# A gated delta rule inside an eight-stage network: new order of its step, and the two stages around it as pipelines

## The chip, the cores and the metric

One NeuronCore of one Trainium2 chip runs the whole network as one program. The metric is the device time of one execution in microseconds, lower is better. All tensors are float32.

## What is computed

Eight layers follow one another, each as `x = x + layernorm(f(layernorm(x)))`, on `x` of shape (8, 512, 128). The change touches only the fifth, the gated delta rule attention. Cut to what matters:

```python
h = silu(conv(rmsnorm(x)) + conv_b)            # causal depthwise convolution, width 4
q, k, v = h @ q_w, h @ k_w, h @ v_w            # 16 heads of 64; q and k normalised
alpha, beta = sigmoid(h @ alpha_w + alpha_b), sigmoid(h @ beta_w + beta_b)
def step(s, inp):                              # scan over 512 tokens, state 64 x 64 per head
    qt, kt, vt, at, bt = inp
    s = s * at[..., None]
    u = einsum('bhd,bhdv->bhv', kt, s)
    s = s + bt * (kt[..., None] * (vt - u)[..., None, :])
    return s, einsum('bhdv,bhd->bhv', s, qt)
y = rmsnorm_per_head(outs)
gate = sigmoid(silu(x @ u1_w + u1_b) @ u2_w + u2_b)
y = x + y @ out_w * gate
y2 = rmsnorm(y)
y = y + silu(y2 @ ff_w1) * (y2 @ ff_w3) @ ff_w2
```

## The kernel before

The core runs eight stages in turn. Between two stages all engines meet at a barrier, and a stage's weights are loaded at its start (`issue_loads`, L102). The fifth layer is three stages. Within a stage each engine runs its own instruction stream in the order written; the streams meet only through semaphores (`wait_ge`, `sem_clear`, `then_inc`).

**The stage ahead, `stage_delta_in` (L1683).** A loop over 8 batches of 512 tokens. VectorE takes the statistics (L130, L133), GpSimd makes the inverse root (L143, L144), VectorE applies it (L155), and the same again for the inner norm (L153). TensorE turns the result (L1721), ScalarE copies it out (L1748), VectorE convolves it in four instructions (L1777, L1779), ScalarE applies SiLU twice (L1754, L1755), TensorE projects the betas in 32 small matmuls (L1730), VectorE adds the bias (L1785), ScalarE applies the sigmoid (L1758), and only then does VectorE begin the next batch. At the end VectorE clears `xn` (L1794).

**The stage of the delta rule, `stage_delta` (L1798).** A loop over 65 turns; one turn, called a step here, is one pair of heads of one batch (8 batches by 8 pairs, and one turn more to end the pipeline). The two heads of a pair lie in the two halves of the 128 partitions, so nearly all matmuls are 64 rows by 64 columns of the array, one head in the quadrant of rows and columns 0 to 63, the other in the quadrant of 64 to 127. The scan is done in chunks of 64 tokens, whose triangular systems are solved by doubling over five levels: at level `l`, `gram(l)` (L2026) forms products of keys, VectorE masks them into `N` and `AT` (`masked`, L2417, L2418), `z_step(l)` (L2055) multiplies `N` by the inverse `T` so far, ScalarE copies `Z` out (L2323), `t_step(l)` (L2069) multiplies again, ScalarE copies `T` (L2316) and VectorE transposes it (L2425). GpSimd scales the keys for the next Gram: `carry(l)` waits for Gram `l`, then scales `kd` (L1914) and `k` (L1908), and its `lv_ready` lets TensorE begin Gram `l + 1`. VectorE hears of a Gram through GpSimd (`gr_fwd`). Between these lie four links of the chain along the sequence: `solve(t)` (L2103 to L2107), copy of `U` (L2329), `state_and_output(t)` (L2117 to L2124), `state(t)` on VectorE (L2437), `from_state(t+1)` (L2137, L2141), `residual` (L2445). The projections of the next step and the output of the one before are spread between them: `project_qk` (L2151), `square_sums` (L2161), `project_gates` (L2167), `key_norms` (L2175), `project_v` (L2182), `head_sums` (L2193), `output` (L2202), and the cross Gram (L2043). At the end of a step are `keys_by_tokens` (L2212), and at its start `gram(0)`, `cross_z` (L2079), `diagonal` (L2014), `cross_t` (L2090). The order on TensorE is the function `step()`. It is written out 5 times (`UNROLL = 5`) in a loop of 13 turns. The other engines loop over single steps.

**The stage behind, `stage_delta_out` (L2567).** A loop over 8 batches: norm of `x`, two gate matmuls (L2614, L2619) with SiLU and sigmoid between them, the gated sum on VectorE (L2692, L2693), inner norm, turn (L2624), four pairs of up products (L2632, L2633), SiLU (L2672), product (L2704), down product (L2641), sum (L2709), the post norm and the sum into `x` (L293). Only the norm of the next batch's input is brought forward.

Of the kernel before, what the change touches and what calls it, by code (L numbers as in the profile page):

```python
# [16 lines left out]
P = 128  # L17
TB = L // P
# [1664 lines left out]
def stage_delta_in(core):  # L1683

    st = Stage(core, "d")
# [3 lines left out]
    pre = Pre(st, inner="rms", eps=DELTA_EPS)  # L1689
    pad = KCONV - 1  # L1690
    hp = st.sb("hp", [P, pad + L])
    cv = st.sb("cv", [P, 2, L])
    hs = st.sb("hs", [P, L])
    bt = st.sb("bt", [P, NC, NPAIR])
    t_ready, t_free = s("pre_t_ready"), s("pre_t_free")
    hp_ready, cv_ready, hs_ready, hs_free = s("conv_in_ready"), s("conv_ready"), s("hs_ready"), s("hs_free")
    b_ps, b_ready, b_done, bank_free = s("beta_ps"), s("beta_ready"), s("beta_done"), s("beta_bank_free")
    with nc.Block() as block:
# [4 lines left out]
        @block.gpsimd  # L1703
        def _(g):
            ch = Chain(g, core.lasting_sem("pool_chain"))
            with g.Fori(0, B) as b:
                ch.reset()
                pre.pool(g, ch, b)

        @block.tensor  # L1710
        def _(pe):
            st.wait_loads(pe)
            pe.sem_inc(pre.y_free, 1)
            pe.sem_inc(hs_free, 1)
            with pe.Fori(0, B) as b:
                pe.wait_ge(pre.y_ready, 1)
                pe.sem_clear(pre.y_ready)
                pe.wait_ge(t_free, 1)
                pe.sem_clear(t_free)
                for t in range(TB):  # L1720
                    r = pe.transpose(c.ps[7][:, t * P:(t + 1) * P], pre.y2[:, t, :], c.ident[:])  # L1721
                r.then_inc(t_ready, 1)
                pe.drain().then_inc(pre.y_free, 1)
                pe.wait_ge(hs_ready, 1)
                pe.sem_clear(hs_ready)
                pe.wait_ge(bank_free, 1)
                pe.sem_clear(bank_free)
                for u in range(NC):
                    for h in range(2):
                        r = pe.matmul(c.psum[h * DH:(h + 1) * DH, 6, u * NPAIR:(u + 1) * NPAIR], hs[:, u * CH:(u + 1) * CH],  # L1730
                                      bw[:, h * NPAIR:(h + 1) * NPAIR], start=True, stop=True)
                r.then_inc(b_ps, 1)
                pe.drain().then_inc(hs_free, 1)
            pe.wait_ge(t_free, 1)
            pe.sem_clear(t_free)
            pe.wait_ge(bank_free, 1)
            pe.sem_clear(bank_free)

        @block.scalar
        def _(a):  # L1740
            ch = Chain(a, core.lasting_sem("act_chain"))
            st.wait_loads(a)
            a.sem_inc(t_free, 1)
            with a.Fori(0, B) as b:
                ch.reset()
                a.wait_ge(t_ready, 1)
                a.sem_clear(t_ready)
                a.activation(hp[:, pad:], c.ps[7], ACT.Identity, scale=gamma[:]).then_inc(hp_ready, 1)  # L1748
                a.drain().then_inc(t_free, 1)
                a.wait_ge(cv_ready, 1)  # L1750
                a.sem_clear(cv_ready)
                a.wait_ge(hs_free, 1)
                a.sem_clear(hs_free)
                a.activation(c.xT[:, bass.ds(b * L, L)], cv[:, 1, :], ACT.Silu, bias=cb[:])  # L1754
                a.activation(hs[:], cv[:, 1, :], ACT.Silu, bias=cb[:]).then_inc(hs_ready, 1)  # L1755
                a.wait_ge(b_ready, 1)
                a.sem_clear(b_ready)
                ch.link(a.activation(c.beta[:, :, bass.ds(b * TB, TB), :],  # L1758
# [1105 lines left out]
```

## Time and profile before

| | |
|---|---|
| median of 3 runs | 6820.89 us (6817.22 to 6825.5) |
| the profiled execution | 6872.23 us, its span 6870.4 us |
| `stage_delta_in` | 182.6 us |
| `stage_delta` | 2717.8 us |
| `stage_delta_out` | 276.9 us |
| the other seven layers | 3693.1 us |
| granted TensorE clock, whole span | 0.869 of 2.4 GHz |

Times are microseconds unless marked ns. PE is TensorE's matmuls, PEld its weight loads, DVE is VectorE, ACT ScalarE, POOL GpSimd. A float32 matmul of the source is two records of the profile, each with its weight load. "Idle before" a record is the time in which that engine had nothing running, with the engine that ended it. A wait for several semaphores is put down to one of them. Matmul ends are modelled, so durations of a group of matmuls are best read from the start of one group to the start of the next.

### The profile page before, as it was taken

What the parts mean: (1) busy time and instruction counts of PE and PEld (TensorE: products, weight loads), DVE (VectorE), ACT (ScalarE), POOL (GpSimd) and SP (SyncE); (2) the same over time, 40 slices, a digit from 0 to 9 for tenths busy, and PEclk for the clock granted to TensorE, in tenths of its full rate; (3) what the DMA queues carried; (4) which work ended last, traced back from release to release, by engine and by line L of the source; (5) the groups of instructions that cost most, each with busy time, mean ns of one, the idle gap of its engine ahead of it and who ended that gap; (6) DMA issues with size and microseconds to landing.
All of it is one profiled execution on the core that took longest, in us unless ns stands there. A gap on an engine that the chain in (4) does not pass through costs nothing.

```text
span 6870.4 us, 180526 instructions
## 1 busy us (share of the span) xinstructions
PE 5324.7 (78%) x70660; PEld 3956.2 (58%) x70660; DVE 3447.2 (50%) x9349; ACT 2368.9 (34%) x4122; POOL 2561.7 (37%) x2842
## 2 busy tenths in 40 slices
PE   4568758888719999999999999997579996111998
PEld 3434435555417877787777787786246664101676
DVE  4531357777634444444444444444445555676433
ACT  3432236666523333333333333333223332000333
POOL 2210014444315555555555556554100002675000
PEclk8789879999859899999999999998789998555999
DMA  0000000000000000000000000000010000000000
GB/s 17 0 17 0 2 37 1 0 0 0 0 6 12 11 11 11 11 11 11 11 11 12 11 10 11 11 13 11 0 37 0 0 0 3 0 0 25 0 0 12
DMA packets 29512, 57.41 MB, mean 8 GB/s; under 512 B 7312, under 2 KB 14240, under 8 KB 28704
## 3 DMA queue, kind: packets, MB, share of 16 engines
q1 hardware_dynamic: 28960, 48.86, 2.2%
q8 instruction: 492, 8.06, 0.5%
q14 instruction: 60, 0.49, 0.0%
HBM read 46.75 MB, written 2.10 MB: 7 GB/s over the span
## 4 chain that ended last, share of the span: by engine, by line
PE 52%; DVE 9%; POOL 3%; another core or an unknown queue 3%; issue 2%; ACT 1%; DVEq 0%; POOLq 0%; ACTq 0%
PE psum L617 7%; PE psum L607 7%; PE psum L2055 5%; PE psum L2026 5%; PE psum L2069 3%; PE psum L600 3%; PE psum L2167 2%; PE psum L2151 2%; PE psum L2161 2%; DVE e_sq L2470 2%; PE psum L2043 1%; POOL a_pv L1480 1%; PE psum L2202 1%; PE psum L2182 1%
## 5 line engine op out<-in xcount | busy, mean ns | idle before, releaser
L617 PEld LDWEIGHTS psum<-m_wd,m_h 128*128 128x128 f32 x6144 | 812.8, 194 | 485.3 <-issue 484.1
L617 PE MATMUL psum<-m_wd,m_h 128*128 128x128 f32 x6144 | 825.5, 278 | 91.2 <-remote 64.4
L1914 POOL TENSOR_TENSOR e_kd<-e_kd,e_tail 128x512 f32<-128x512 f32 x325 | 369.5, 1137 | 694.1 <-PE psum L2026 680.8
L607 PE MATMUL psum<-xT,m_wa 128*128 (+1 forms) x1032 | 552.7, 618 | 8.5 <-remote 8.5
L607 PE MATMUL psum<-xT,m_wb 128*128 (+1 forms) x1032 | 540.4, 606 | 0.0
L784 DVE SCALAR_TENSOR_TENSOR m_acc<-psum,m_combine,m_acc 128x128 f32<-128x128 f32 x1440 | 403.4, 342 | 223.3 <-PE psum L617 209.5
L544 POOL TENSOR_TENSOR m_h<-m_td,m_tb 128x512 f32<-128x512 f32 x258 | 328.5, 1273 | 487.1 <-DVE m_tb L812 487.1
L2055 PEld LDWEIGHTS psum<-e_T,e_N 64*64 64x64 f32 x10400 | 336.0, 137 | 217.6 <-issue 216.6
L2026 PE MATMUL psum<-e_kd,e_k 64*64 64x64 f32 x10400 | 375.7, 223 | 49.4 <-DVE e_AT L2418 49.3
L2055 PE MATMUL psum<-e_T,e_N 64*64 64x32 f32 x10400 | 371.9, 222 | 43.6 <-remote 43.6
L2026 PEld LDWEIGHTS psum<-e_kd,e_k 64*64 64x64 f32 x10400 | 343.5, 138 | 57.8 <-issue 56.4
L143 POOL TENSOR_SCALAR m_post_rstd<-m_post_mv 128x4 f32<-128x4 f32 x27 | 6.1, 228 | 991.5 <-DVE m_post_mv L133 991.5
L607 PEld LDWEIGHTS psum<-xT,m_wb 128*128 128x128 f32 x1032 | 202.6, 196 | 258.5 <-issue 258.5
L805 DVE SCALAR_TENSOR_TENSOR m_h<-psum,m_bb,m_ta 128x512 f32<-128x512 f32 x258 | 193.2, 749 | 309.4 <-ACT m_ta L705 306.2
L705 ACT ACTIVATE m_ta<-psum,m_ba 128x512 f32<-128x512 f32 x258 | 177.2, 687 | 459.7 <-PE psum L607 459.6
L1908 POOL TENSOR_TENSOR e_k<-e_k,e_tail 128x256 f32<-128x256 f32 x390 | 283.4, 727 | 121.9 <-PE psum L2043 121.9
L2323 ACT ACTIVATE e_Z<-psum 128x256 f32<-128x256 f32 x325 | 124.5, 383 | 574.5 <-PE psum L2055 572.0
L2316 ACT ACTIVATE e_T<-psum 128x256 f32<-128x256 f32 x325 | 126.0, 388 | 556.7 <-PE psum L2069 556.7
L2069 PE MATMUL psum<-e_Z,e_TT 64*64 64x32 f32 x8320 | 283.8, 219 | 0.0
L2069 PEld LDWEIGHTS psum<-e_Z,e_TT 64*64 64x64 f32 x8320 | 276.6, 136 | 4.4
L699 ACT ACTIVATE m_h<-psum,m_ba 128x512 f32<-128x512 f32 x258 | 177.3, 687 | 287.0 <-PE psum L600 287.0
L600 PE MATMUL psum<-m_normed,m_wa 128*128 128x512 f32 x516 | 268.5, 603 | 6.3 <-remote 6.3
(412 smaller groups left out, 11727.5 us busy)
## 6 DMA issues: line engine op xcount, KB each, us to landing
e_w<-in_e_w SPq DMA_DIRECT2D x66, 321.0 KB, 2.8
m_wa<-in_m_wa SPq DMA_DIRECT2D x12, 512.0 KB, 7.2
m_wd<-in_m_wd SPq DMA_DIRECT2D x12, 512.0 KB, 8.7
m_wb<-in_m_wb SPq DMA_DIRECT2D x8, 512.0 KB, 9.0
f_h<-in_f_h SPq DMA_DIRECT2D x2, 1024.0 KB
out<-x SPq DMA_DIRECT2D x1, 2048.0 KB, 8.7
f_w<-in_f_w SPq DMA_DIRECT2D x3, 256.0 KB
g_w<-in_g_w SPq DMA_DIRECT2D x3, 256.0 KB
```

The lines of the kernel that those rows point to most:

```text
L544: g.tensor_tensor(h[:, j, :], td[:, j, :], tb[:, j, :], ALU.mult).then_inc(h_ready[j], 1)
L600: pe.matmul(c.ps[u % 4][:], wa[q][:, j, :], nrm[:, e % 2, :], start=True, stop=True).then_inc(a_ready[u % 4], 1)
L607: pe.matmul(c.ps[i][:], w[q][:, j, :], xb, start=True, stop=True).then_inc(a_ready[i], 1)
L617: r = pe.matmul(c.ps[4 + e % 2][:, t * P:(t + 1) * P], h[:, u % DEPTH, t * P:(t + 1) * P], wd[u // UQ][:, u % UQ, :], start=(m == 0 and t ...
L699: a.activation(h[:, j, :], c.ps[u % 4][:], ACT.Relu, bias=ba[:, u:u + 1]).then_inc(h_ready[j], 1)
L784: r = v.scalar_tensor_tensor(to[:, t, :], c.ps[4 + e % 2][:, t * P:(t + 1) * P], comb[:, t, e:e + 1], acc[:, t, :], ALU.mult, ALU.add)
L805: v.scalar_tensor_tensor(h[:, j, :], c.ps[2 * k + 1][:], bb[:, u:u + 1], ta[:, j, :], ALU.add, ALU.mult).then_inc(h_ready[j], 1)
L1908: return g.tensor_tensor(even(k[:], m), even(src[:], m), gate, ALU.mult)
L1914: return g.tensor_tensor(both_odd(dst[:], m), both_odd(src[:], m), gate.unsqueeze(1).broadcast_to((P, 2, nb, m)), ALU.mult)
L2026: r = pe.matmul(c.psum[half(h), G_, chunk(u)], keys[half(h), chunk(u)], both_odd(gated[half(h), :, chunk(u)], m), start=True, stop=True)
L2055: r = pe.matmul(c.psum[half(h), Z_, u * HC:(u + 1) * HC], N[half(h), l - 1, chunk(u)], even(T[half(h), chunk(u)], 1 << l), start=True, sto ...
L2069: r = pe.matmul(even(c.psum[half(h), T_, chunk(u)], 1 << l), left[half(h), chunk(u)], Z[half(h), u, :], start=False, stop=False, skip_grou ...
```

## The change

**Stage ahead.** The loop over batches is written out as a pipeline. Buffers are doubled (`hp`, `cv`, `y2`, two PSUM banks each for turning and betas). VectorE interleaves the first norm of batch `b + 2`, the second part of batch `b + 1` and the convolution of batch `b`. SiLU is applied once, and the betas are projected from `xT`. One sigmoid over all batches at the end takes the place of eight. `xn` is cleared on GpSimd.

**The step.** `z_step(l)` and `gram(l + 1)` (for `l = 5` the cross Gram) become one function `z_and_gram(l)`, whose matmuls alternate. `Z` of a head is written to the other half of the PSUM partitions, so it uses the quadrants that the Gram leaves free. ScalarE copies one half of `Z` back, VectorE the other. The order of the step on TensorE, ScalarE and VectorE is new, and `UNROLL` is 13.

**Stage behind.** The loop is written out. First all gates of the 8 batches are made, with one sigmoid over all; then the gated sums run on GpSimd, three batches ahead; up products run one batch ahead of down products.

```diff
-    UNROLL = 5
+    UNROLL = 13
...
+            def z_and_gram(l):
+
+                pe.wait_ge(n_ready, 1)
+                pe.sem_clear(n_ready)
+                pe.wait_ge(t_ready, 1)
+                pe.sem_clear(t_ready)
                 pe.wait_ge(lv_ready, 1)
                 pe.sem_clear(lv_ready)
                 pe.wait_ge(gr_free, 1)
                 pe.sem_clear(gr_free)
...
                 for u in range(NC):
                     for h in range(2):
-                        r = pe.matmul(c.psum[half(h), Z_, u * HC:(u + 1) * HC], N[half(h), l - 1, chunk(u)],
+                        r = pe.matmul(c.psum[half(1 - h), Z_, u * HC:(u + 1) * HC], N[half(h), l - 1, chunk(u)],
                                       even(T[half(h), chunk(u)], 1 << l), start=True, stop=True)
-                r.then_inc(z_ps, 1)
+                        if u + 1 == NC:
+                            r.then_inc(z_ps[h], 1)
+                    if l + 1 < LEVELS:
+                        r = gram_chunk(l + 1, k, kd, u)
+                    elif u % 2:
+                        r = cross_block(u // 2)
+                r.then_inc(gr_ps, 1)
...
-                scaled_gram(1)
+                gram(1, k, kd, gr_free, gr_ps)
                 solve(0)
-                z_step(1)
                 state_and_output(0)
-                scaled_gram(2)
                 from_state(1)
+                z_and_gram(1)
+                solve(1)
                 t_step(1)
-                solve(1)
                 pe.wait_ge(out_free, 1)
                 pe.sem_clear(out_free)
                 project_qk()
-                z_step(2)
                 state_and_output(1)
-                scaled_gram(3)
                 from_state(2)
+                z_and_gram(2)
+                square_sums()
                 t_step(2)
                 solve(2)
-                square_sums()
+                z_and_gram(3)
                 project_gates()
...
+            def z_copy():
+
+                v.wait_ge(z_ps[1], 1)
+                v.sem_clear(z_ps[1])
+                v.tensor_copy(flat(Z[half(1)]), c.psum[half(0), Z_, 0:NC * HC]).then_inc(z_ready[1], 1)
```

VectorE's loop in the stage ahead, and TensorE's in the stage behind, after the change:

```python
            for b in range(B):
                if b + 1 < B:
                    third(b + 1)
                if b + 2 < B:
                    first(b + 2)
                conv(b)
                if b + 2 < B:
                    second(b + 2)
                if b >= 1:
                    betas(b - 1)
...
            for b in range(B):
                if b + 1 < B:
                    up(b + 1)
                if b + 2 < B:
                    turn_sums(b + 2)
                down(b)
```

## Rows read from the trace of the kernel before

**Rows 1.** Busy time by stage: start:end, length, busy and count, clock, DMA

```profile
1859.20:2041.80 182.60, 23.94 (x288) 20.06 (x288) 66.25 (x250) 39.21 (x48) 20.22 (x32) 0.50 0.00 0
2041.80:4759.60 2717.80, 2470.59 (x55182) 2136.09 (x55182) 1265.79 (x3082) 921.26 (x2020) 1580.62 (x1909) 0.92 0.04 11
4759.60:5036.50 276.90, 139.82 (x532) 81.55 (x532) 109.64 (x388) 75.65 (x98) 31.60 (x50) 0.71 0.01 3
```

**Rows 2.** Timeline of a batch in the stage ahead: start, length, record, idle before

```profile
1885.50 0.87 DVE L130 BATCH_NORM_STATS2 d_pre_stats<-x 128x6 f32 x4 [2.68 <-remote]
1888.47 1.12 DVE L155 TENSOR_SCALAR d_pre_y<-x,d_pre_mv,d_pre_rstd 128x128 f32 x4 [1.69 <-POOL d_pre_rstd L144]
1896.76 2.33 DVE L1779 SCALAR_TENSOR_TENSOR d_cv<-d_hp,d_cw,d_cv 128x512 f32<-128x512 f32 x3
1902.30 1.89 PE L1730 MATMUL psum<-d_betaw,d_hs 128*64 128x8 f32 x32 [7.01 <-remote]
```

**Rows 3.** VectorE's copy of TX, once a step: all 65, and two neighbours

```profile
L2512 DVE COPY e_TX<-psum x65: 424/443/459, 2082.2 to 4721.4; 128x256 f32<-128x256 f32 x65
...
3278.43 0.45 DVE L2512 COPY e_TX<-psum 128x256 f32<-128x256 f32 x1
...
3326.75 0.42 DVE L2512 COPY e_TX<-psum 128x256 f32<-128x256 f32 x1 [1.30 <-PE psum L2090]
```

**Rows 4.** Chain that ended last, where TensorE's loop turns: start, length, what

```profile
3315.48 4.37 another core or an unknown queue
...
3321.70 1.02 issue
```

**Rows 5.** Timeline of one step: TensorE's waits, and GpSimd's carry

```profile
2161.57 1.15 PE L2026 MATMUL psum<-e_kd,e_k 64*64 64x64 f32 x32 [0.93 <-DVE e_AT L2418]
2162.99 1.29 POOL L1914 TENSOR_TENSOR e_kd<-e_kd,e_tail 128x512 f32<-128x512 f32 x1 [1.15 <-PE psum L2026]
2163.70 1.12 PE L2055 MATMUL psum<-e_T,e_N 64*64 64x32 f32 x32 [0.64 <-remote]
2164.24 0.74 POOL L1908 TENSOR_TENSOR e_k<-e_k,e_tail 128x256 f32<-128x256 f32 x1
2164.65 0.43 PE L2117 MATMUL psum<-e_U,e_ket 64*64 64x64 f32 x8
2170.76 1.02 ACT L2293 ACTIVATE e_sq<-psum 128x1024 f32<-128x1024 f32 x1 [1.83 <-PE psum L2151]
2183.59 0.33 PE L2103 MATMUL psum<-e_bv,e_TTH 64*64 64x64 f32 x4 [0.84 <-DVE e_bv L2445]
```

**Rows 6.** Matmuls of other stages on several tiles; the third row is L1002 alone

```profile
73.63 1.09 PE L1002 MATMUL psum<-a_kz,a_qT 64*32 64x512 f32 x16
74.65 0.74 PE L1022 MATMUL psum<-a_vz,a_probsT 128*32 128x18 f32 x64
73.70:73.80 0.10, 0.10 (x8) 0.10 (x16) 1.00 0.00 0
```

**Rows 7.** Busy time and clock (the third number from the end) of three short stretches

```profile
3319.90:3325.90 6.00, 4.94 (x89) 4.85 (x91) 2.08 (x3) 1.42 (x3) 0.00 (x0) 0.50 0.02 5
3381.60:3385.00 3.40, 3.40 (x5) 1.16 (x5) 0.17 (x1) 0.00 (x0) 2.76 (x1) 0.54 0.00 0
2176.80:2178.70 1.90, 1.90 (x6) 0.70 (x5) 0.17 (x1) 0.00 (x0) 1.22 (x1) 1.00 0.00 0
```

**Rows 8.** Timeline of the stage behind: its start, and one batch

```profile
4766.96 0.87 DVE L130 BATCH_NORM_STATS2 g_pre_stats<-x 128x6 f32<-128x128 f32 x4 [7.80 <-DMA g_gamma<-in_g_gamma]
...
4798.40 1.02 PE L2632 MATMUL psum<-g_y2T,g_w 128*128 128x512 f32 x2
...
4799.26 1.02 PE L2633 MATMUL psum<-g_y2T,g_w 128*128 128x512 f32 x2
...
4801.64 3.83 PE L2641 MATMUL psum<-g_w,g_hid 128*128 128x128 f32 x32 [0.92 <-remote]
```

**Rows 9.** Groups by shape in the stage behind: busy, mean ns, idle before

```profile
L2664 ACT ACT_TABLE_LOAD x8 | 10.3, 1283 | 32.3 <-DVE g_gate L2688 32.3
```

More of the change, by code:

```diff
@@ L1739, in _ @@
+                r.then_inc(b_ps[i], 1)
+            turn(0)
+            for b in range(B):
+                if b + 1 < B:
+                    turn(b + 1)
+                betas(b)
+            for i in range(2):
+                pe.wait_ge(b_read[i], 1)
+                pe.sem_clear(b_read[i])
         @block.scalar
         def _(a):
-            ch = Chain(a, core.lasting_sem("act_chain"))
             st.wait_loads(a)
[L1743 to L1758, printed above, removed]
-                                     bt[:].rearrange("p (t h) a -> p a t h", h=2), ACT.Sigmoid))
-                a.sem_inc(b_done, 1)
@@ new lines, in betas @@
+            def betas(b):
+                i = b % 2
+                v.wait_ge(b_ps[i], 1)
+                v.sem_clear(b_ps[i])
+                r = v.tensor_tensor(bt[:, b * NC:(b + 1) * NC, :], c.ps[6 + i][:, 0:NC * NPAIR].rearrange("p (u a) -> p u a", u=NC),
+                                    bb[:].unsqueeze(1).broadcast_to((P, NC, NPAIR)), ALU.add)
+                r.then_inc(b_read[i], 1)
+                return r
+            first(0)
+            second(0)
+            third(0)
+            first(1)
@@ L1795, in stage_delta_in @@
+            second(1)
+            for b in range(B):
+                if b + 1 < B:
+                    third(b + 1)
[6 more added lines that the diff above has]
+                    betas(b - 1)
+            betas(B - 1)
+            v.drain().then_inc(b_ready, 1)
     st.ctx.close()
@@ L2644, in _ @@
+            up(0)
+            turn_sums(1)
+            for b in range(B):
+                if b + 1 < B:
+                    up(b + 1)
+                if b + 2 < B:
+                    turn_sums(b + 2)
+                down(b)
             for i in range(2):
@@ L2675, in _ @@
+            copy_sums(0)
+            for b in range(B):
+                silus(b)
+                if b + 1 < B:
+                    copy_sums(b + 1)
         @block.vector
@@ new lines, in _ @@
+            gate_sum(B - 2)
+            gate_sum(B - 1)
+            sums_stats(0)
+            sums_norm(0)
+            sums_stats(1)
+            hidden(0)
+            sums_norm(1)
+            sums_stats(2)
+            for b in range(B):
+                if b + 1 < B:
+                    hidden(b + 1)
+                if b + 2 < B:
+                    sums_norm(b + 2)
+                if b:
+                    finish(b - 1)
+                result(b)
+                if b + 3 < B:
+                    sums_stats(b + 3)
```

501 lines of the change are left out of this document (286 added, 215 removed).

## The prediction

> **What bounds the kernel now.** I read the busy times by stage first [rows 1]. Three stages are touched: 182.6, 2717.8 and 276.9 us, 3177.3 of 6870.4. The seven other layers' 3693.1 us stay. The reader is to see two kinds of stage. In the stage ahead and the one behind no engine is busy: 66 of 182.6 us for the busiest in the first, 140 of 276.9 in the last, with the clock at 0.50 and 0.71. They are chains of single instructions, each waiting for the one before. In the delta stage TensorE is busy 2471 of 2718 us, so what shortens it is TensorE work or TensorE's waits.
>
> Next I read the timeline of one batch [rows 2, 8], the times of one recurring instruction [rows 3], and the chain of waits through a step and over the turn of the loop [rows 4]. The copy of TX is seen 65 times from 2082.2 to 4721.4, 41.24 us a step. Of the 64 intervals between neighbours, 52 are inside TensorE's loop body, 37.4 to 42.4 us with mean 39.6. The 12 at the turn of its loop are 45.1 to 50.2, mean 48.2; one is 3278.43 to 3326.75. There the chain shows 4.37 and 1.02 us in which TensorE has nothing to run [rows 4], and the six microseconds after it have a clock of 0.50 [rows 7]. A turn thus costs 48.2 - 39.6 = 8.6 us.
>
> **The stage ahead.** One batch's work on VectorE is, from starts in the timeline: first norm's statistics 1.3 (0.87 and 0.38 with gaps), its application and the second statistics 2.8, second application 1.0, convolution 2.9 (0.48 + 2.33), beta sum 0.3: 8.3 us. What goes is the round trip: TensorE's 7.01 us and its kin, one SiLU [rows 2], and 7 sigmoids with their 1.28 us table loads, as in [rows 9]. GpSimd's root takes 1.69 us from statistics to application. `first` is covered by the convolution, but `third(b+1)` comes right after `second` and `betas`, so 1.69 - 0.33 = 1.3 us of it stays each time. Prologue: 1.3 + 1.7 + 2.8 + 1.7 + 1.0 + 1.3 + 1.7 + 2.8 = 14.3. Six full turns of 9.6 = 57.6. The last two batches 5.5 + 3.2. The end (SiLU, 1.89 of TensorE, bias, table 1.28, a sigmoid of 512 columns 0.7) 5.9. Loads at the start 3.6. Sum 90 against 182.6: **92 us gone**, 80 to 102 by whether the roots are hidden and whether GpSimd's clearing of `xn` (3.5 us on VectorE before) holds up its second root.
>
> **The stage behind.** Loads 7.4 us [rows 8]. Gates of 8 batches: VectorE needs 1.3 + 1.1 + 0.7 and 0.5 of root wait, 3.6 a batch; TensorE's turn and two products 2.8 at the full clock, 5.0 at half. I take 4.3, 34 in all, and 5 of fill. One sigmoid of 4096 columns: 0.42 us for each 512 (the ScalarE record of 1024 columns is 1.02 [rows 5], that of 512 0.60) and a table load 1.28 [rows 9], 4.9. Then gated sum 2.6 on GpSimd (1.27 each), statistics 1.9, root 1.7, application 0.9, turn 1.3, copy 0.9: 9.3. First up products, clock half low, 8.5. From there TensorE sets the pace: 7 up products of 8 x 0.86 (4798.40 to 4799.26) = 48.2, 8 down products of 3.8 = 30.4, turns 3.6. VectorE does `result` and `sums_stats` (3.9 us) behind each down product before it frees the banks that the third pair of up products waits for; four matmuls (3.4) cover part, and 1.5 us a batch stays, 10.5. Tail 6.3. Sum 168: **109 us gone**, 150 to 200 by the clock.
>
> **The step: matmuls beside one another.** Z is 32 records and a Gram 32, and each takes 0.94 to 0.98 us from start to start (2163.70 to 2164.65 in [rows 5]), 29 ns a record, whether 32 or 64 columns stream. So a pair of quadrants is bound by its own loads and streams, not by columns. Is it the quadrants or the issue of instructions? Two rows of the first layer tell: 64 records of 128 x 32 begin and end in 0.74 us, at most 12 ns each; and L1002, on 2 x 4 tiles of 64 x 32, has 8 matmuls and 16 weight loads in the same 0.1 us, and ends 16 records of 512 columns in 1.09 us [rows 6]. Issue allows 12 ns, and tiles in both rows and columns run together. Z then hides beside the Gram: 1.0 us for both instead of 1.9. No row has four tiles of 64 x 64, so the bounds are 0.94 (each quadrant's own time) and 1.9 (no gain). I take 1.0, being nearest to L1002. Five times a step: 4.5 us less TensorE work.
>
> The Trainium skill (TensorEngine Tiling (Array Packing), Gotcha 1: PSUM Pressure) speaks against it: different row tiles cannot access the same PSUM bank at once. Both heads' Z lie in one bank, as both heads' Gram do. By that rule the two heads of the old Gram would take turns; but two records of 512 columns in a row on one tile fit in L1002's 1.09 us, so 64 columns stream in 55 to 68 ns, and 29 ns a record is possible only when the heads run together. With four tiles the rule could still bind, and give the first rival below.
>
> **The step: waits.** TensorE's waits in a plain step of 38.16 us are 1.06 before Gram 1 (it shows as 0.93), 0.79 before Z, 0.84 before solve 3 and some 0.6 in small ones [rows 5], 3.3 in all, so 34.9 of work; less 4.5 is 30.4. Now each link of the sequence loses the work that covered it. I walked the new order, Gram 1 at 0, with the latencies of the rows: 0.44 from TensorE to GpSimd, 0.28 to 0.30 to ScalarE, 0.39 to VectorE's `state`, 0.15 to 0.28 back. Gram 1 ends at 0.98, solve 0 at 1.33; the U copy ends at 1.89, so the state products begin at 2.09 (0.76 idle); S is copied by 2.93, `from_state(1)` runs 3.08 to 3.53 (0.4 idle). GpSimd's two scalings (1.29 + 0.74) end at 3.41, and `z_and_gram(1)` begins at 3.69 (0.16). Its Z copies take until 5.5, solve 1 covers part (0.5). The output sums free the banks at 6.6 (0.2 before `project_qk`). `from_state(2)` waits 0.44 for S; `z_and_gram(3)` comes 0.5 early for T 2, `from_state(3)` 0.44 for S, `z_and_gram(4)` 0.5 for T 3. From there to the end nothing waits. Before Gram 1 the old 0.9 stays, since its chain (ket, k, GpSimd 0.84 + 1.50) is unchanged and the diagonal behind `cross_t` fills the wait. Sum 4.8; two more changes between tile shapes, 0.15 each. Step: 30.4 + 4.8 + 0.3 = 35.4. GpSimd's work a step is near 25 us and VectorE's 22, so neither becomes the bound.
>
> **The clock.** Plain intervals without a slow phase are near 38.1, and the mean is 39.6, so slow phases cost 1.5 us a step: the gate products behind the square sums take 3.4 us at a clock of 0.54 and 1.9 at 1.00 [rows 7]. The square sums and head sums stay, so I keep 1.5, between 0 and 4: denser matmuls and more gaps pull both ways. Step 36.9.
>
> **UNROLL** 13 leaves 5 turns of the loop, 4 jumps back instead of 12: 8 x 8.6 = 69 us. Its cover is none, it stands on TensorE's path. The Trainium skill (Runtime: NRT & Kernel Launch, Instruction fetch mechanics) says that a taken branch outside the buffered pages must fetch first; the trace agrees, with 4.37 us at each turn and none within the 5 steps.
>
> Delta stage: 64 x 36.9 = 2362, 4 x 8.6 = 34, the start and last step 76: 2472, **246 us gone**.
>
> **Sum.** 92 + 109 + 246 = 447. The profiled execution was 6872.2 (1.8 around its span), so 6425; it is 51 us above the median of the runs, so 6374 us in the median. Its own range by the bounds (step 33.9 to 38.9, which is 128 us either way at most, the stages 20 and 30) is 6270 to 6500.
>
> **Rivals.** (1) *Four quadrants do not overlap.* The pair stays at 1.9, some 0.3 of waits are covered by it, step 41.1, stage 64 x 41.1 + 34 + 78 = 2742, 24 more than before. With the two outer stages: 6872 + 24 - 201 - 51 = 6644. For it: no row with this shape, and the page's rule. Against: L1002. (2) *The gaps let the clock fall.* After the idle at the loop's turn everything runs at half clock for 6 us [rows 7]. The new step has gaps of 0.4 to 0.8 in its first 7 us. The step must reach (2718 + 201 - 34 - 78) / 64 = 43.9 us for the whole to be slower: 7.0 more than I say, 14 us more of each step at 1.2 GHz. At 45 us it would be 6890. Against: gaps of 0.6 to 0.9 follow each other already at Gram 1 and Z, and that stretch has a full clock. (3) *Only the outer stages gain less*, because unrolled code and GpSimd's gated sums keep their chains: 60 and 60 instead of 92 and 109 would give 6455; this lies in the range.
>
> **How the numbers follow.** My forecast with its range 0.70 (of which a twentieth below 6290), the first rival or a partial overlap 6500 to 6660 0.24, the second 0.04, anything that ends within noise 0.02. The range takes in the first rival: 6270 to 6660. Faster by over 0.2% (13.6 us, what this measurement can tell) 0.94, within 0.01, slower 0.05; the second rival makes nearly all of the last.
>
> **What would show it.** `z_and_gram` in 1.0 us for 64 records, against 1.9; TX copies 36.9 apart, four of them with about 8.6 more; the stage ahead in 90 and the one behind in 168 us; waits of 0.4 to 0.8 before the state products and `from_state`. The forecast fails if the records beside each other stay at 29 ns, if the clock in the stage falls well under 0.92, or if another engine's wait (VectorE's half of the Z copy stands behind `residual` and, at level 2, behind `rest`) holds up every level.

## The result and the profile after

The changed kernel takes 6558.68 us in the median (6549.27 to 6568.25, 4 runs) against 6823.19 (6817.22 to 6829.8, 4 runs): a ratio of 0.9612, 95% interval 0.9595 to 0.963. That is 264 us faster, where 447 were forecast; it lies inside the stated range (6270 to 6660), 185 us above its point. It lies above 6500, where the forecast's own range ended; the range reached further only to take in the first rival, and that rival did not occur.

The profiled execution has a span of 6566.4 us. By stage (start:end, length, busy time and count of PE, PEld, DVE, ACT, POOL, then clock, DMA share, GB/s), answering to [rows 1]:

```profile
1849.40:1940.00 90.60, 23.95 (x288) 20.07 (x288) 63.02 (x248) 14.96 (x19) 28.02 (x34) 0.50 0.01 1
1940.00:4479.70 2539.70, 2249.34 (x55182) 1823.45 (x55182) 1487.52 (x3407) 912.50 (x2020) 1605.25 (x1909) 0.93 0.04 12
4479.70:4736.10 256.40, 158.27 (x528) 93.69 (x528) 96.40 (x360) 42.20 (x60) 51.17 (x64) 0.71 0.01 4
```

The stage ahead fell from 182.6 to 90.6 us, as forecast (90). The delta stage fell by 178 us, not 246. The stage behind, forecast at 168, is 256.4, only 20.5 less than before, although VectorE, ScalarE and GpSimd together have 27 us less to do in it. The other layers are 3679.7 us, 13 less, with no edit in them. Over the traces of all kernels here they take some 3677 to 3697 us, so these 13 are scatter.

The recurring copy of TX in the changed kernel (min/median/max ns, first and last start), answering to [rows 3]:

```profile
L2564 DVE COPY e_TX<-psum x65: 424/447/471, 1978.8 to 4440.7; 128x256 f32<-128x256 f32 x65
```

Its 64 intervals fall into 60 inside the loop body, 35.96 to 40.62 us with mean 38.04 (before 39.6), and 4 at a turn, mean 44.81, so a turn now costs 6.8 us. The forecast had 36.9 and 8.6.

One pair of Z and Gram on TensorE in the changed kernel (start, length, line, tile), answering to the Gram and Z of [rows 5], which took one after the other what is here in one:

```profile
2747.19 0.25 PE L2097 MATMUL psum<-e_T,e_N 64*64 64x32 f32 x2
2747.20 0.27 PE L2067 MATMUL psum<-e_kd,e_k 64*64 64x64 f32 x2
...
2748.13 0.23 PE L2067 MATMUL psum<-e_kd,e_k 64*64 64x64 f32 x2
2748.18 0.28 PE L2152 MATMUL psum<-e_bv,e_TTH 64*64 64x64 f32 x4
```

From 2747.19 to 2748.18 are 0.99 us for 64 records, 15.5 ns each. Forecast: 1.0. The pairs of the higher levels take 1.09 to 1.10 us at the full clock; a group of another tile shape follows each of them.

Where the stage behind lost its gain is seen in two stretches. First its loop over the gates in the changed kernel, one round:

```profile
4511.13 1.11 PE L2690 MATMUL psum<-ident,g_y 128*128 128x128 f32 x4 [3.41 <-DVE g_y L155]
4512.17 1.97 PE L2697 MATMUL psum<-g_xTs,g_u 128*64 128x512 f32 x2
4514.07 2.07 PE L2707 MATMUL psum<-g_u,g_g 64*128 64x128 f32 x8
4516.29 0.69 DVE L2834 TENSOR_TENSOR g_gate<-psum,g_u2b 128x512 f32<-128x512 f32 x1 [5.31 <-PE psum L2707]
4518.32 1.08 DVE L155 TENSOR_SCALAR g_y<-x,g_pre_mv,g_pre_rstd 128x128 f32<-128x128 f32 x4
4519.55 1.11 PE L2690 MATMUL psum<-ident,g_y 128*128 128x128 f32 x4 [3.41 <-DVE g_y L155]
```

The reader is to see a closed ring of 8.42 us (4511.13 to 4519.55). VectorE's gate sum waits 5.31 us for a product that TensorE runs only after the turn of this same round, and the next turn waits for what VectorE does after the gate sum. The granted clock over this round is 0.50, and the matmuls are about twice as long as at the full clock: 1.97 us for two records of 128 x 512, which take 1.02 in the next rows.

Then the main loop of that stage, the middle of batch 0, where the third pair of up products should follow the second at once:

```profile
4597.22 1.02 PE L2726 MATMUL psum<-g_y2T,g_w 128*128 128x512 f32 x2
4597.47 1.04 POOL L144 TENSOR_TENSOR g_post_rstd<-g_post_rstd,mhalf 128x4 f32<-128x4 f32 x1
...
4598.48 1.26 POOL L2665 TENSOR_TENSOR g_gate<-g_gate,xn 128x512 f32<-128x512 f32 x1
4599.82 1.26 POOL L2666 TENSOR_TENSOR g_y<-g_y,g_gate 128x512 f32<-128x512 f32 x1
4601.12 0.87 DVE L130 BATCH_NORM_STATS2 g_inner_stats<-g_y 128x6 f32<-128x128 f32 x4 [4.15 <-POOL g_y L2666]
...
4602.85 0.69 DVE L2852 TENSOR_TENSOR g_hid<-psum,g_silu 128x512 f32<-128x512 f32 x1
...
4603.76 2.07 PE L2725 MATMUL psum<-g_y2T,g_w 128*128 128x512 f32 x2 [5.52 <-DVEq L2853]
4605.62 1.91 PE L2726 MATMUL psum<-g_y2T,g_w 128*128 128x512 f32 x2
```

TensorE stands 5.52 us for the bank that VectorE's product (L2852) frees. VectorE stands before that in the statistics of batch 3's gated sum, 4.15 us, for GpSimd. GpSimd began the sum only after the root of batch 0's post norm, which itself needs `result(0)`. After that stand the up products take 1.91 and 2.07 where they took 1.02, and the granted clock from 4603.76 to 4610.00 is 0.55. The down products start at 4589.97, 4613.24, 4636.89, 4660.65, 4684.49 and 4708.34: some 23.7 us a batch, where the forecast's terms make 12.8 (6.9 for the up products, 3.8 for the down product, 0.6 for the turn, 1.5 for VectorE).

### The profile page after: what moved, and what is told of

Its sections match the earlier page's. It is cut to its first block and busy times, and to the rows that moved or that the text cites. A ratio compares the mean times of both kernels' runs of the same rounds, so it can differ in the third digit from the quotient of the medians.

```text
span 6566.4 us, 180965 instructions
## 1 busy us (share of the span) xinstructions
PE 5106.9 (78%) x70656; PEld 3646.3 (56%) x70656; DVE 3654.6 (56%) x9644; ACT 2302.8 (35%) x4055; POOL 2614.5 (40%) x2858
## 5 line engine op out<-in xcount | busy, mean ns | idle before, releaser
L2097 PE MATMUL psum<-e_T,e_N 64*64 64x32 f32 x10400 | 406.7, 232 | 66.1 <-remote 64.1
L2097 PEld LDWEIGHTS psum<-e_T,e_N 64*64 64x64 f32 x10400 | 370.1, 148 | 113.6 <-issue 110.6
L2067 PE MATMUL psum<-e_kd,e_k 64*64 64x64 f32 x10400 | 419.4, 236 | 1.7 <-issue 1.2
L2067 PEld LDWEIGHTS psum<-e_kd,e_k 64*64 64x64 f32 x10400 | 371.7, 148 | 7.7 <-issue 1.1
L2118 PE MATMUL psum<-e_Z,e_TT 64*64 64x32 f32 x8320 | 300.5, 222 | 27.5 <-DVE e_Z L2470 22.6
L2470 DVE COPY e_Z<-psum 64x256 f32<-64x256 f32 x325 | 135.8, 418 | 303.7 <-PE psum L2097 302.9
```

Source lines behind the costliest of these rows:

```text
L2067: r = pe.matmul(c.psum[half(h), G_, chunk(u)], keys[half(h), chunk(u)], both_odd(gated[half(h), :, chunk(u)], 1 << l), start=True, stop=True)
L2097: r = pe.matmul(c.psum[half(1 - h), Z_, u * HC:(u + 1) * HC], N[half(h), l - 1, chunk(u)], even(T[half(h), chunk(u)], 1 << l), start=True, ...
L2118: r = pe.matmul(even(c.psum[half(h), T_, chunk(u)], 1 << l), left[half(h), chunk(u)], Z[half(h), u, :], start=False, stop=False, skip_grou ...
```

## The experiments

Twelve kernels ran, in four groups (runs 1 to 4, 5 to 8, 9 and 10, 11 and 12), each group on one chip; the median of the kernel before lay between 6820.0 and 6824.3 us in them. Gains "over the changed kernel" are against 6558.7.

**1. GpSimd's gated sum first.** In `stage_delta_out`:

```diff
 # GpSimd
-                post.pool(g, ch)
                 if b + 3 < B:
                     gated(b + 3)
                     norm.pool_rstd(g, ch)
+                post.pool(g, ch)
 # VectorE
-                result(b)
                 if b + 3 < B:
                     sums_stats(b + 3)
+                result(b)
```

> The changed kernel, but in the main loop of the stage behind GpSimd makes the gated hidden values of batch b+3 ahead of the root of batch b's post norm, and VectorE reads their statistics ahead of result(b). Changed kernel: 23.6 us a batch over batches 0 to 4, stage 256.4 us. Theory (VectorE stands in the statistics of b+3 until GpSimd's gated product lands, the next up pair stands behind it, and TensorE's clock falls in that gap): a batch falls to 15 to 18 us, so the stage goes to 220 to 230 us and the kernel is 25 to 40 us faster than the changed kernel. Rival 1 (the clock is the limit whatever the order, the gap moves elsewhere): a batch stays above 21 us and the kernel within 10 us of the changed one. Rival 2 (the down products behind the turned sums are the gap): 2 to 3 us a batch at most from this edit, 10 to 15 us in all.

Measured: 6512.29 us, 46 less. The down products of this kernel:

```profile
4568.44 3.74 PE L2736 MATMUL psum<-g_w,g_hid 128*128 128x128 f32 x32
...
4581.85 3.74 PE L2736 MATMUL psum<-g_w,g_hid 128*128 128x128 f32 x32
```

That is 13.41 us a batch, less than the theory itself expected, and near the forecast's 12.8 (the five intervals are 13.4 to 14.6); the stage is 200.7 us. Both rivals fall. The gap did not move elsewhere: the stand of 5.52 us is gone, and TensorE's longest wait in a batch is the 2.31 us ahead of the turned sums, which the changed kernel has too. From the first down product to the sixth the granted clock is 0.98, where it was 0.79.

**2. The gate sum one batch later.** VectorE's input loop:

```diff
-                if b >= 2:
-                    gate_sum(b - 2)
+                if b >= 3:
+                    gate_sum(b - 3)
+            gate_sum(B - 3)
```

> The changed kernel, but in the input loop of the stage behind VectorE sums the gates of batch b-3 where it summed those of b-2, and the last one after the loop. Changed kernel: 8.42 us a batch in a ring of VectorE norm, TensorE turn_input, gate_up, gate_down, VectorE gate sum, next norm. Theory (the ring is closed by the gate sum that waits for a product of the same round): a batch falls to the longer of VectorE's own work and TensorE's own work at half clock, about 5 to 6 us, so 8 batches give 16 to 25 us. Rival (each round is bound by TensorE at half clock or by the input transfers): the round stays above 7.5 us, under 8 us gained in all.

Measured: 6532.16 us, 27 less. The stretch from the first turn to the last gate sum, in the changed kernel and then in this one:

```profile
4491.10:4546.80 55.70, 37.34 (x112) 20.89 (x112) 19.92 (x84) 11.40 (x17) 8.31 (x13) 0.56 0.00 1
```

```profile
4487.90:4515.20 27.30, 24.76 (x112) 13.69 (x112) 18.89 (x83) 11.40 (x17) 8.25 (x13) 0.86 0.00 1
```

The ring was the cause, and the theory was too small: rounds are 2.7 to 3.9 us (three of the turns are at 4496.84, 4500.31 and 4503.33), since with the gaps gone the granted clock rose from 0.56 to 0.86. TensorE at half clock was no limit of its own, but a result of the ring.

**3. The old kernel with `UNROLL = 13`**, in place of 5.

> The kernel before with 13 pairs of tokens in a turn of its step loop in place of 5, so 4 turns between tokens in place of 12; nothing else. By the prediction's price (8.6 us a turn over a plain step) 8 turns less give 69 us: 6754 us. By the price of the turns that are left in the changed kernel (6.8 us) 54 us: 6769 us. Rival (a longer body costs as much in fetching instructions as the turns did): no change.

Measured: 6763.7 us (6758.05 to 6790.08), a ratio of 0.9922 (0.9898 to 0.9946) to the kernel before: 60 us against the 6823.9 of this group, 7.5 a turn. The interval of the ratio is 37 to 70 us, so it excludes the rival but does not decide between the two prices. In this kernel's own trace the 4 turns have mean 45.90 among plain steps of 39.23, 6.7 a turn.

**4. Z in its own half.** The only edit is which half of the partitions holds it:

```diff
-  r = pe.matmul(c.psum[half(1 - h), Z_, u * HC:(u + 1) * HC], N[half(h), l - 1, chunk(u)],
+  r = pe.matmul(c.psum[half(h), Z_, u * HC:(u + 1) * HC], N[half(h), l - 1, chunk(u)],
```

and the two copies read the half that they write.

> The changed kernel with the order of its matmuls kept, but each head's Z written to its own half of the partitions, so that Z and the Gram beside it no longer lie in opposite quadrants. Theory (records in opposite quadrants overlap, and this alone makes a pair last 0.99 us): a pair lasts 1.8 to 1.9 us, the step grows by 3 to 4.5 us, the kernel by 190 to 290 us. Rival (the pair is short because its operands are ready, and the step is bound by its chain between the engines): a pair stays near 1.0 to 1.2 us and the kernel within 60 us of the changed one.

Measured: 6922.96 us, 364 more than the changed kernel, and a ratio of 1.0138 (1.0108 to 1.0169) to the kernel before. One pair in this kernel, of which the first and the last rows stand:

```profile
2740.00 0.30 PE L2097 MATMUL psum<-e_T,e_N 64*64 64x32 f32 x4
2740.13 0.32 PE L2067 MATMUL psum<-e_kd,e_k 64*64 64x64 f32 x4
...
2741.68 0.26 PE L2097 MATMUL psum<-e_T,e_N 64*64 64x32 f32 x4
2741.77 0.32 PE L2067 MATMUL psum<-e_kd,e_k 64*64 64x64 f32 x4
2742.01 1.95 PE L2210 MATMUL psum<-e_headmask,e_sq 128*128 128x2 f32 x16
```

From 2740.00 to 2742.01 are 2.01 us; the changed kernel's pair at this place, ahead of the square sums, takes 1.09. The first pair of a step takes 1.91 us (30 ns a record), where the changed kernel has 0.99 in the same order of instructions. This is the forecast's first rival as a kernel. Its shortest plain step is 40.13 us (rival: 41.1), but its mean is 43.55, and the clock between the first and last TX copy is 0.90 in place of 0.94. Against the changed kernel the shortest step is 4.2 us longer, as the theory has it, and the mean 5.5. The difference goes with the longer stretches at half clock (543 us in all against 300), which the theory had not priced.

**5. All Z records, then all of the Gram.** The same quadrants as the changed kernel, one more line in `z_and_gram`:

```diff
                 for u in range(NC):
                     for h in range(2):
                         r = pe.matmul(c.psum[half(1 - h), Z_, ...
+                for u in range(NC):
                     if l + 1 < LEVELS:
                         r = gram_chunk(l + 1, k, kd, u)
```

> The changed kernel, but of each pair of Z and Gram TensorE issues the 32 records of Z first and then the 32 of the Gram; both still lie in their own quadrants. Theory (records overlap only where neighbours in the queue lie in quadrants that share neither rows nor columns): inside Z the heads alternate between two quadrants as before the change, so a pair goes back to 1.8 to 1.9 us and the kernel to the time of the run in which Z lay in its own half, 200 to 360 us above the changed kernel. Rival (four quadrants are merely used as a pool, any order will do, since neighbours of both heads lie in two different quadrants already): a pair stays at 1.0 to 1.1 us and the kernel within 40 us of the changed one.

Measured: 6803.03 us, 244 more. The pair of the last level in this kernel:

```profile
2763.80 0.95 PE L2097 MATMUL psum<-e_T,e_N 64*64 64x32 f32 x26
...
2764.80 0.82 PE L2081 MATMUL psum<-e_kd,e_k 64*64 64x128 f32 x12
2765.55 1.16 PE L2252 MATMUL psum<-e_owp,e_y 64*128 64x128 f32 x16
```

1.75 us to the next group, where the changed kernel's cross pair takes 1.10; the first pair of a step takes 1.72 in place of 0.99. Four quadrants are of use only if the queue goes round all of them. Free quadrants alone are worth little, 0.2 us a pair (1.91 in run 4). The theory's wording, neighbours that share neither rows nor columns, is stricter than what helped: in the changed kernel each record of `Z` of head 1 and the Gram record of head 0 behind it write the same half of the partitions, so they share columns. What the three orders show is a time for each quadrant. An estimate from them: one quadrant takes a record every 54 to 62 ns, with two in turn (2 x 27 in run 5, 2 x 30 in run 4) as with four (4 x 15.5).

**6. The changed kernel with `UNROLL = 5`.**

> The changed kernel with 5 pairs of tokens in a turn of its step loop in place of 13: 12 turns between tokens in place of 4, as the kernel before has. At 6.8 us a turn over a plain step, as the changed kernel's 4 turns show, 8 turns more cost 54 us: 6613 us; at the prediction's 8.6 us 69 us: 6628 us. Rival (the turn's cost is hidden behind the new order): under 20 us.

Measured: 6620.21 us, 61.5 more, 7.7 a turn. Its own trace has 12 turns of mean 45.27 among 52 plain steps of 37.86: 7.4. Both figures of the expectation are near, and the rival falls.

**7. The down products ahead of the turned sums**, on top of run 1:

```diff
+                down(b)
                 if b + 2 < B:
                     turn_sums(b + 2)
-                down(b)
```

> The kernel in which GpSimd makes the gated values of batch b+3 ahead of batch b's post root (13.4 us a batch), and TensorE's down(b) ahead of turn_sums(b+2) as well. There TensorE idles 2.3 us a batch ahead of turn_sums(b+2), with down(b) ready behind it. Theory (that idle time is on the ring): 1.5 to 2.3 us a batch less over 6 batches, 9 to 14 us in all. Rival (the ring closes over VectorE and GpSimd, so TensorE only idles elsewhere, or up(b+2) is reached later): within 4 us.

Measured: 6500.95 us, 11 less than run 1; the down products are 12.2 us apart, 1.2 us a batch less, and the stage is 192.1 us. The 2.31 us of idle time were on the ring, half of them. The single executions of the two kernels overlap (6498.2 to 6518.0 and 6498.3 to 6507.4 us), so the size rests on the traces, where the stage is 8.6 us shorter.

**8. All three edits of the stage behind.**

> The changed kernel with all three edits of the stage behind: gates of b-3 summed in the input loop (-26 us alone), GpSimd's gated values ahead of the post root (-46 us alone), and down(b) ahead of turn_sums(b+2). Theory (the first two lie in different phases of the stage and add up): 6558.7 - 26.5 - 46.4 = 6486 us, with the third edit up to 14 us less. Rival (they share a cover, such as the clock, which has to rise in either phase): 6500 us or more.

Measured: 6473.07 us, 86 less than the changed kernel, as the theory has it; the rival falls. The stage in this kernel:

```profile
4485.70:4651.50 165.80, 117.71 (x528) 71.55 (x528) 95.23 (x360) 42.18 (x60) 51.20 (x64) 0.87 0.02 6
```

165.8 us, where the forecast for the change as it stood was 168, with the same instructions as in the changed kernel. TensorE is busy for 118 us in place of 158.

**9. Square and head sums over 64 columns.** The mask of the heads has two columns; here 62 more of zeros, so that the 12 small products of a step (24 records, 16 of square sums and 8 of head sums) stream more:

```diff
-    ones, hm = st.sb("ones", [P, DH]), st.sb("headmask", [P, 2])
+    ones, hm = st.sb("ones", [P, DH]), st.sb("headmask", [P, 64])
...
-  r = pe.matmul(c.ps[X_][:, at:at + 2], sq[:, n, block(t)], hm[:], start=True, stop=True)
+  r = pe.matmul(c.ps[X_][:, at:at + 64], sq[:, n, block(t)], hm[:], start=True, stop=True)
...
-  r = pe.matmul(c.ps[X_][:, 2 * t:2 * t + 2], ysq[:, block(t)], hm[:], start=True, stop=True)
+  r = pe.matmul(c.ps[X_][:, 2 * t:2 * t + 64], ysq[:, block(t)], hm[:], start=True, stop=True)
```

> The changed kernel, but the products that sum squares over a head's rows (16 square sums and 4 head sums a step) run over 64 columns, 62 of them zeros, in place of 2; nothing else reads the further columns. In the changed kernel a step's 16 square sums take 1.95 us for 32 columns in all, and in the step walked the granted clock falls from 1.00 to 0.50 some 2 us after them, for 3 to 4 us. Theory (the stretch with hardly a column is what the clock falls after, and its slow phase is what the forecast of a step lacks beyond its waits): with the same issue time the slow phase shrinks or is gone, a plain step falls from 38.0 to 36.2 to 37.0 us, and the kernel is 60 to 110 us faster. Rival 1 (the clock falls after the waits between the engines, whatever the width): steps keep 37.8 to 38.2 us. Rival 2 (64 columns make the square sums longer than their weight loads): steps grow by 0.3 to 1.5 us, 20 to 90 us slower.

Measured: 6472.54 us, 86 less than the changed kernel. One step in windows; first the changed kernel: up to the square sums, the square sums, the T step and solve after them, the third pair and the gate products, the rest:

```profile
2743.46:2755.38 11.92, 10.07 (x277) 7.80 (x277) 6.79 (x19) 3.82 (x8) 4.85 (x7) 1.00 0.01 3
2755.38:2757.25 1.87, 1.87 (x22) 1.86 (x16) 1.37 (x4) 0.38 (x1) 1.54 (x2) 1.00 0.00 0
2757.25:2759.28 2.03, 1.51 (x46) 1.37 (x45) 0.39 (x2) 0.58 (x2) 1.62 (x2) 1.00 0.03 8
2759.28:2762.82 3.54, 3.54 (x66) 2.63 (x67) 1.89 (x4) 0.08 (x1) 2.77 (x3) 0.52 0.02 5
2762.82:2781.32 18.50, 16.87 (x448) 14.09 (x446) 12.28 (x26) 9.13 (x20) 13.80 (x19) 1.00 0.07 20
```

Then the same stretches of a step with 64 columns:

```profile
2844.61:2846.53 1.92, 1.92 (x22) 1.86 (x16) 1.37 (x4) 0.38 (x1) 1.59 (x2) 1.00 0.00 0
2846.53:2848.60 2.07, 1.54 (x49) 1.41 (x48) 0.43 (x2) 0.62 (x2) 1.60 (x2) 1.00 0.00 0
2848.60:2852.20 3.60, 3.60 (x84) 2.29 (x84) 2.32 (x5) 0.49 (x2) 3.04 (x3) 1.00 0.02 5
```

The square sums take the same time (1.92 against 1.87), the wait after them is the same, and the clock stays at 1.00. The plain steps have a median of 36.24 us and a mean of 36.69 in place of 37.79 and 38.04. The whole traces agree with the one step: in the changed kernel a stretch at half clock begins 13.5 to 19.6 us after the TX copy in 56 of the 64 steps, in this one in none. Ten such stretches are left in it, 4 at the turns and 6 elsewhere, so the few columns are not the only thing that the clock falls after. TensorE's busy time is full in either version of the square sums, so the profile's busy share did not point here; only the clock's column, read stretch by stretch, did.

**10. All three edits of the stage behind, all 65 steps written out.**

> The kernel with all three edits of the stage behind (6473 us), with all 65 steps written out, so that no turn of the loop is left between tokens. At 6.7 us a turn as its own trace shows (44.9 less 38.1), the 4 turns left cost 27 us: 6446 us. Rival (four more bodies of instructions to fetch in one run stall the engines as much): no gain.

Measured: 6449.67 us, 23 less than run 8; plain steps have mean 37.9 and none is over 40.5.

**11. The kernel before with 64 columns.** The edit of run 9 on the old order.

> The kernel before with its square and head sums over 64 columns in place of 2, as in the run on the changed kernel (86 us faster there). Theory (the same stretch of few columns lowered the clock in the order before too, where a plain step's mean is 39.6 us and its shortest 37.35 us): a plain step falls to 37.7 to 38.5 us, 60 to 120 us faster, so the clock was a cost of both kernels and no part of what the change did. Rival (in the order before the records that stood beside the sums kept the clock up, and only the new order, with Z and Gram in half the time, lets it fall): under 30 us.

Measured: 6759.88 us, 60 less, a ratio of 0.9896 (0.9874 to 0.9919). Its plain steps fall from 39.6 to 38.07 (the 39.6 are of an execution 49 us above its kernel's median), and the clock from the first to the last TX copy rises from 0.93 to 0.98. In the trace of before the clock falls at two places of a step: 13.5 to 19.6 us after the TX copy, by the square sums, in 23 steps, and 30 to 33.2 us after it, behind the head sums, in 36. In this kernel it falls at neither. Square sums and head sums were not widened apart. The old order bore this cost as well, some two thirds of it: a piece of it stood in [rows 7], the gate products behind the square sums in 3.4 us at 0.54. The gain is at the low end of what the theory expected.

**12. All edits together:** stage behind, no turns, 64 columns.

> All edits together: the three of the stage behind, 65 steps written out, and the square and head sums over 64 columns. If the gains add: 6449.7 (all edits but the width) less 86.1 (the width alone, 6558.7 less 6472.5) = 6364 us. Theory (they lie in different places: stage behind, turns, TensorE's clock within a step): 6355 to 6375 us. Rival (the turns' price was partly the slow clock after the stall, which the width already shortened, so that part is counted twice): 6375 to 6395 us.

Measured: 6358.43 us (6350.72 to 6363.03, 5 runs), a ratio of 0.9309 (0.9285 to 0.9333) to the kernel before. The gains add; the rival falls. The delta stage between the first and the last TX copy of this kernel, and of the changed one:

```profile
1987.30:4324.58 2337.28, 2084.04 (x54280) 1702.21 (x54277) 1456.76 (x3330) 895.22 (x1984) 1558.78 (x1855) 1.00 0.04 12
```

```profile
1978.83:4440.69 2461.86, 2195.78 (x54280) 1785.81 (x54277) 1453.88 (x3328) 895.14 (x1984) 1563.71 (x1855) 0.94 0.04 12
```

The number of TensorE's instructions is the same; they take 112 us less, with the clock at 1.00 in place of 0.94.

## Why the prediction was right, and where its terms were off

The sum was made against the profiled execution of before, 6872.2 us; that of the changed kernel is 6568.2. So 304 us are gone of the 447. By the medians the gain is 264: the profiled execution of before lay 49 us above its median and that of the changed kernel 10 above. Some 40 of the 304 us are thus scatter between two executions, 13.4 of them in the other layers. The stages ahead and behind keep their lengths within 1 us in the traces of runs 3 and 11, where they are unedited, so the other 26 are most likely in the delta stage, whose gain is then some 150 us.

| term | forecast | measured |
|---|---|---|
| stage ahead | 92 gone | 92.0 |
| stage behind | 109 gone | 20.5 |
| delta stage | 246 gone | 178.1 |
| rest of the network | 0 | 13.4 (scatter) |

**Stage ahead: right.** 90.6 us against a walk of 90, still at clock 0.50. The agreement within 1 us is in part luck, since two errors cancel. The rounds are 9.3 us, not 9.6, 2 us less in six. The part ahead of them takes 17.1 us, not 14.3, and here the clearing of `xn` counts: it did not delay GpSimd's root but ran beside VectorE's second application, which took 3.86 us where the same line takes 0.88 later (that the one slowed the other was not tested apart):

```profile
1860.28 3.51 POOL L1720 MEMSET xn<- 128x4096 f32 x1
1860.47 3.86 DVE L153 TENSOR_SCALAR d_y<-d_y,d_inner_rstd 128x128 f32<-128x128 f32 x4 [1.68 <-POOL d_inner_rstd L144]
...
1871.71 0.88 DVE L153 TENSOR_SCALAR d_y<-d_y,d_inner_rstd 128x128 f32<-128x128 f32 x4 [1.68 <-POOL d_inner_rstd L144]
```

**Stage behind: the step that failed, in two of its terms.** (a) "Gates of 8 batches: I take 4.3" a batch compared VectorE's own work with TensorE's, and left out that the gate sum of batch b - 2 needs a product that TensorE has queued after the turn of batch b. The ring took 8.42 us; run 2 opened it, and the rounds became 2.7 to 3.9. (b) "VectorE does `result` and `sums_stats` (3.9 us) behind each down product" took `sums_stats` as work, though it is a wait: for GpSimd's gated sum, queued behind the root of the post norm, which waits for `result`. The term of 1.5 us a batch for VectorE became a stand of 5.5 us on TensorE, and a clock of 0.55 after it. Run 1 took this wait away and brought a batch from 23.7 to 13.4 us; run 7 took away another that the forecast left out, the down products behind the turned sums. With all of it the stage is 165.8 us. So the forecast of 168 was that of a pipeline whose queues are in the right order, and the change's were not. The third rival named this mechanism ("GpSimd's gated sums keep their chains") and priced the stage at 60 gone; it was worse. What it said of the stage ahead, 60 gone in place of 92, did not occur.

**Delta stage: the mechanism right, two sizes off.** The pair at 1.0 us is 0.99 to 1.10, and runs 4 and 5 show that the gain of the step hangs on it: 364 us more without the opposite quadrants, 244 more without the alternation. Against the old order with the same 4 turns (run 3, 6763.7), the changed kernel has 205 us less, of which the two outer stages are 112; about 93 are left for the new order and the overlap, 1.4 us a step. The new order without the overlap (run 4) is slower than the old one, and pays only with it.

The Trainium skill's rule that weighed against it (TensorEngine Tiling (Array Packing), Gotcha 1: PSUM Pressure: row tiles cannot access one PSUM bank at once) shows no cost in time here: both heads' Z go to one bank, at 15.5 ns a record over the four quadrants.

The plain step was to be 35.4 us clean and 1.5 for the clock. Clean steps are 36.3 us in the mean (51 steps of run 9 that have the full clock throughout; shortest 35.9). TensorE's waits in the step of the changed kernel that was walked, Gram 1 at 2743.46:

```profile
2741.84 0.68 PE L2139 MATMUL psum<-e_TTH,e_ZX 64*64 64x64 f32 x16 [0.79 <-DVE e_TTH L2481]
...
2745.51 0.45 PE L2166 MATMUL psum<-e_U,e_ket 64*64 64x64 f32 x8 [0.56 <-ACT e_U L2375]
...
2746.49 0.45 PE L2186 MATMUL psum<-e_S,e_kdH 64*64 64x64 f32 x8 [0.19 <-DVE e_S L2489]
...
2749.08 0.58 PE L2118 MATMUL psum<-e_Z,e_TT 64*64 64x32 f32 x13 [0.38 <-DVE e_Z L2470]
2750.03 0.77 PE L2118 MATMUL psum<-e_Z,e_TT 64*64 64x32 f32 x19 [0.37 <-issue]
```

The walk held to within 0.05 us up to `z_and_gram(1)` (2.09, 3.08 and 3.69 forecast; 2.05, 3.03 and 3.73 measured) and to about 0.1 at the first T step. It missed the 0.37 us gap inside that step. "From there to the end nothing waits" missed 0.79 us before `cross_t`; but the old 0.9 before Gram 1, which the walk kept, is gone, so this wait only moved. What is missing is in the work. At the full clock a step of before waits 2.5 us by the profile and is busy for 35.5 (mean of 12 steps); in the last kernel it waits 3.9 and is busy for 32.4 (59 steps), and the changed kernel's 5 such steps have the same busy time. The waits grew by 1.4 us, for 1.5 in the forecast (3.3 to 4.8); the busy time fell by 3.1, for 4.2 (4.5 less 0.3). The five pairs gave 4.2 of their 4.5. But the state products take 2.8 us a step in place of 2.2 and `from_state` 1.9 in place of 1.4. Their records are the same. In the old order a Gram or a T step began some 0.2 us before their last records had ended; in the new one the group behind begins only when they have. For the state products the cause is plain, since the group behind waits for what they feed; for `from_state` it is not shown. The term "34.9 of work; less 4.5" took the work of a record as the same in any order.

The clock cost 38.04 - 36.3 = 1.7 us, near the 1.5 taken over from the old kernel, but it was no constant: run 9 removes most of it, in all 86 us, and run 11 removes 60 of the old kernel's. "The square sums and head sums stay, so I keep 1.5" had the cause in it and did not ask what it would be worth to touch it. The steps thus give 64 x (38.04 - 36.9) = 73 us of what is missing.

**UNROLL: right, priced a little high.** Forecast 8.6 us a turn; runs 3 and 6 give 7.5 and 7.7 from medians, and the turns left in the changed kernel 6.8. Run 10 takes them away, for 23 us. The 4.37 us "at each turn" are those of the one turn read: over the 12 turns of the trace of before the wait is 3.0 to 4.8 us, and none of 3 us stands within the 5 steps.

**The rivals.** The first did not occur, and as a kernel (run 4) it is slower than before, not 6644. Its price took the stage behind at 168 and 1.5 us of slow clock a step, where run 4 has 3.4 between its shortest and its mean plain step. The second, that gaps lower the clock, does not hold for the gaps it named: run 9 keeps the waits of 0.2 to 0.8 us, and in the step shown the clock stays at its upper level. For longer gaps it holds in part. The clock falls at every turn of the loop, and in the last kernel, where neither turn nor narrow product is left, it falls in 5 steps; in 4 of them TensorE stood for 1.2 to 1.4 us, until 1 to 2 us before the fall. In 4 other steps it stood as long and the clock did not fall.

**How the range came to hold.** It held by luck. The measured 6559 lies above the own range of the forecast, and the 6500 to 6660 beyond it stood for four quadrants that do not overlap, or overlap in part; they overlap fully, and what filled this part of the range was the stage behind (88 us less gone than forecast) and the longer steps of the delta stage (68 us by the traces). The sums of the range are also off. The step's lower bound, 33.9, is 3.0 us below 36.9, which is 192 us over 64 steps and not 128; and with 128 for the steps and 50 for the stages, the upper end would be 6552, not 6500. The step's terms add up to 35.5, not 35.4.

## What to carry to other kernels

When a loop is turned into a pipeline by hand, the work of each engine does not tell the round time. Write down, for each queue, what the item that waits is behind, and follow it around until the ring closes; three changes in the order of queues were worth 90 us in a stage of 256. In that stage a gap on TensorE was paid twice, once as a wait and once as half clock after it.

Independent small matmuls in different quadrants ran beside one another only when they alternated in the queue; test the placement and the alternation apart. A group moved to where its result is awaited no longer hides its last records behind the next group. And look for what precedes each slow stretch of the clock: here it was a run of products with two columns each, which cost nothing to widen.

## What was not expected of the hardware

- Sixteen records of 128 x 128 by 2 columns take 1.87 us and by 64 columns 1.92, so the width was free; but the wide ones kept TensorE's clock at 1.00 where it had fallen to 0.52, worth 86 us in the changed kernel and 60 in the one before.
- Records in four quadrants of 64 x 64, alternating, start 15.5 ns apart on average; two quadrants reach 30 ns, in the same order of instructions. The Trainium skill (TensorE: Matmul & The Clock Gate, Wait — 56ns, not 53.3ns?) gives about 25 ns as the least from start to start; the trace has less over several tiles, 15.5 here.
- Closing the gaps of a loop gave more than the gaps: TensorE's busy time for the same 528 instructions of the stage behind fell from 158.27 to 117.71 us.
- In the last kernel the plain steps still differ, 35.9 to 38.7 us. The five above 38 us (38.2 to 38.7) are the five in which the clock falls, once each, for 3.4 us, 8.3 to 9.2 us after the TX copy. The other 59 have the full clock throughout and take 35.9 to 37.5 us; why these differ is open.
- Also open: why the same wait of 1.2 to 1.4 us, which comes in every eighth step of the last kernel inside `solve(1)` with nothing that the profile shows as its cause, comes ahead of a fall of the clock in 4 of 8 steps and not in the others.
